# ACT's copies moved behind a period's second exp, POOL's power behind the split of x, and the scores split expert by expert, in a fused attention and expert-routing kernel

## What is computed

```
x   = _layernorm(x)                          # 16 sequences of 512 tokens, 256 wide
out = x0 + attention(x) + expert_ffn(x)      # x0 is the input
attention: q, k = rms_norm(x Wq'), rms_norm(x Wk'); v = x Wv'   # 16 heads of 16
           softmax(q k' / 4) v, then Wo'
expert_ffn: norm = layer_norm(x); scores = norm @ centroids.T    # 8192 tokens x 8 experts
           for e in 0..7: the 1024 best tokens by scores[:, e] that no expert before e has taken
           for each expert's tokens: routed + gelu(layer_norm(routed) w1 + b1) w2 + b2
           scattered back to the tokens' own rows
```

## Time and profile before

| | |
|---|---|
| median of three runs | 1113.92 us |
| the profiled execution | 1116.27 us, span 1114.5 us |
| mean granted TensorE clock | 0.979 |
| PE busy | 1052.2 us (94%) |
| DVE busy | 829.7 us (74%) |
| ACT busy | 745.0 us (67%) |
| POOL busy | 728.9 us (65%) |
| the chain that ended last | PE 69%, DVE 8%, issue 7%, POOL 5%, DMA 4%, ACT 4% |

### The profile page before, as it was taken

The page is one execution under the profiler, slowest core; times in us unless marked ns, Lnnn a source line. Parts: engine busy times, 40 slices in busy tenths (PEclk is TensorE's granted clock), DMA queues, the critical chain, the costliest instruction groups (busy, mean ns, idle before and its releaser), DMA issues.

```text
span 1114.5 us, 20949 instructions
## 1 busy us (share of the span) xinstructions
PE 1052.2 (94%) x7222; PEld 680.0 (61%) x7222; DVE 829.7 (74%) x1846; ACT 745.0 (67%) x966; POOL 728.9 (65%) x762
## 2 busy tenths in 40 slices
PE   4799999899999999999999987899999999999997
PEld 3445555444444444454454442388999889998897
DVE  8799896577777687677878787587677686776861
ACT  3488887678888878888888874675445554554550
POOL 5577877566775866777676667646676656767334
PEclk9899999999999999999999996999999999999999
DMA  4866977558577776766765966314344343444313
GB/s 142 188 143 143 219 159 154 114 132 162 125 155 148 158 138 123 179 129 139 161 136 136 166 154 129 105 57 119 81 89 122 60 119 81 85 104 77 68 20 38
DMA packets 86361, 138.16 MB, mean 124 GB/s; under 512 B 12768, under 2 KB 38624, under 8 KB 86240
## 3 DMA queue, kind: packets, MB, share of 16 engines
q1 hardware_dynamic: 57392, 103.06, 41.5%
q0 software_dynamic: 12288, 16.79, 9.0%
q10 hardware_dynamic: 16560, 16.78, 5.7%
HBM read 86.25 MB, written 50.33 MB: 123 GB/s over the span
## 4 chain that ended last, share of the span: by engine, by line
PE 69%; DVE 8%; issue 7%; POOL 5%; DMA 4%; ACT 4%; SPq 2%; ACTq 0%; POOLq 0%; another core or an unknown queue 0%; DVEq 0%
PE W L1443 16%; PE S L1429 15%; PE pv L485 13%; PE S L470 10%; PE W L431 7%; DMA stq<-parts 4%; PE W L442 3%; ACT prob L677 2%; SPq L316 2%; PE W L456 2%; DMA parts<-hi 1%; POOL hi L1186 1%; DVE raw L807 1%; PE pv L1415 1%; PE R L1415 1%
## 5 line engine op out<-in xcount | busy, mean ns | idle before, releaser
L677 ACT ACTIVATE prob<-S 128x1024 f32<-128x1024 f32 x512 | 498.1, 1022 | 132.6 <-PE S L470 131.0
L485 PE MATMUL pv<-prob,v 128*17 128x512 f32 x2048 | 252.5, 611 | 2.4 <-DVE oT L840 2.4
L470 PE MATMUL S<-stq,stk 64*128 64x512 f32 x1024 | 202.2, 460 | 24.7 <-ACT prob L677 15.4
L470 PEld LDWEIGHTS S<-stq,stk 64*128 64x128 f32 x1024 | 84.6, 186 | 150.9 <-ACT prob L677 110.5
L1705 POOL DMA_INDIRECT out<-prob,order_rows x64 | 105.8, 1653 | 48.0 <-DVE prob L1645 37.1
L485 PEld LDWEIGHTS pv<-prob,v 128*17 128x17 f32 x2048 | 48.0, 97 | 125.1 <-issue 119.2
L1156 POOL TENSOR_TENSOR sq<-raw 128x512 f32<-128x512 f32 x62 | 64.4, 1040 | 87.3 <-DVE raw L807 55.9
L1505 ACT ACTIVATE wq_act<-S,b 128x512 f32<-128x512 f32 x64 | 43.9, 687 | 94.7 <-PE S L1429 89.1
L1429 PE MATMUL S<-raw_nT,xT_w 128*128 128x512 f32 x384 | 91.1, 395 | 1.8 <-DVE raw_nT L1623 1.8
L1429 PEld LDWEIGHTS S<-raw_nT,xT_w 128*128 128x128 f32 x384 | 71.6, 188 | 19.6 <-issue 3.6
L1190 POOL TENSOR_TENSOR lo<-full,hi 128x512 fp32r<-128x512 f32 x62 | 79.9, 1289 | 5.0
(11 more groups left out here) (253 smaller groups left out, 2649.1 us busy)
## 6 DMA issues: line engine op xcount, KB each, us to landing
stk<-parts SPq DMA_DIRECT2D x192, 128.0 KB, 4.3
stq<-parts SPq DMA_DIRECT2D x192, 128.0 KB, 6.6
xT<-in_w SPq DMA_DIRECT2D x32, 512.0 KB
parts<-hi SPq DMA_DIRECT2D x63, 256.0 KB, 2.1
parts<-lo SPq DMA_DIRECT2D x63, 256.0 KB, 2.0
out<-ao ACTq DMA_DIRECT2D x32, 256.0 KB, 5.6
xb<-in_x ACTq DMA_DIRECT2D x13, 512.0 KB, 5.3
xb<-in_x SPq DMA_DIRECT2D x2, 512.0 KB, 5.7
```

The source lines that it names most:

```text
L470: ins = e.matmul(S[n % 2][:, h, :], stack["k"][u][64 * h:64 * h + 64, p, c * P:(c + 1) * P], stack["q"][u][64 * h:64 * h + 64, p, :], star ...
L485: ins = e.matmul(pv[32 * j:32 * j + VW, :], v[b % 2][:, c, 8 * u + 4 * g + j, :], prob[(2 * t + j // 2) % RING][:, j % 2, :], start=(c == ...
L677: e.activation(prob[n % RING][:, :, :], S[n % 2][:, :, :], ACT.Exp).then_inc(s_exp, 1)
```

## The change

Three things are moved, and no arithmetic is changed. On ACT, in a period, `evict_xT`, `load_x` and `evict_o` stood ahead of the period's first exp and `put_out` behind the second; now all of them stand behind the second exp, in the order second half of x, load, first half of x, output copy, output DMA. On POOL, `second_power` stood second in a period and now stands behind `split_x`. On DVE, the split of the scores' bits is made for one expert's 128x64 columns at a time: expert 0 at period 32, and the next expert's in the seventh period of each expert (`i == 6`).

```diff
@@ scalar_program @@
             for kk in range(PERIODS):
                 at = PERIODS * b + kk
-                if scored(at - 2) is not None:
-                    evict_xT(e, scored(at - 2), 0)
-                if scored(at - 3) is not None:
-                    evict_xT(e, scored(at - 3), 1)
-                    if scored(at - 3) + XB < B:
-                        load_x(e, scored(at - 3) + XB)
-                if b and kk in (5, 6):
-                    evict_o(e, b - 1, kk - 5)
                 softmax(e, 4 * at)
                 for u in range(2):
                     if nb < B and squares_at(nb, u) + 1 == at:
                         inverse_rms(e, nb, u)
                 softmax(e, 4 * at + 1)
+                if scored(at - 3) is not None:
+                    evict_xT(e, scored(at - 3), 1)
+                    if scored(at - 3) + XB < B:
+                        load_x(e, scored(at - 3) + XB)
+                if scored(at - 2) is not None:
+                    evict_xT(e, scored(at - 2), 0)
                 if b and kk in (5, 6):
+                    evict_o(e, b - 1, kk - 5)
                     put_out(e, b - 1, kk - 5)
                 softmax(e, 4 * at + 2)
                 softmax(e, 4 * at + 3)
@@ split_scores, vector_program @@
-    def split_scores(e):
+    def split_scores(e, ex):
...
-        e.tensor_scalar(word, words.bitcast(I32), 31, 1, ALU.arith_shift_right, ALU.logical_shift_right).then_inc(r_split, 1)
+        bits, words, parts = (t[:, ex, :] for t in (word, scores.bitcast(I32), part))
+        if ex == 0:
+            e.wait_ge(s_score, B)
+        e.tensor_scalar(bits, words, 31, 1, ALU.arith_shift_right, ALU.logical_shift_right).then_inc(r_split, 1)
...
                 if at == ROUTE:
-                    split_scores(e)
+                    split_scores(e, 0)
...
+                if routed(at)[1] == 6 and ex < E - 2:
+                    split_scores(e, ex + 1)
@@ gpsimd_program @@
                 if scored(at) is not None:
                     first_power(e, scored(at))
-                if scored(at - 1) is not None:
-                    second_power(e, scored(at - 1))
...
                 if b + 2 < B and kk == 5:
                     split_x(e, b + 2)
+                if scored(at - 1) is not None:
+                    second_power(e, scored(at - 1))
```

More of the change, by code:

```diff
@@ L275, in attention_and_routing @@
     hot_e = [xb[0][:, i, :].bitcast(BF16).rearrange("p (t q) -> p t q", t=COLS) for i in range(2)]
-    word = xb[0][:, 0:2, :].rearrange("p c d -> p (c d)").bitcast(I32)
-    part = xb[1][:, 0:2, :].rearrange("p c d -> p (c d)").bitcast(I32)
+    word = xb[0][:, 0:2, :].rearrange("p c d -> p (c d)").bitcast(I32).rearrange("p (e t) -> p e t", e=E)
+    part = xb[1][:, 0:2, :].rearrange("p c d -> p (c d)").bitcast(I32).rearrange("p (e t) -> p e t", e=E)
     low = xb[2][:, 0:2, :].rearrange("p c d -> p (c d)").rearrange("p (e t) -> p e t", e=E)
@@ L863, in shift_vector @@
         e.tensor_tensor(sh[1][:, :], shf[:, :], sh[0][:, :].bitcast(F32), ALU.subtract).then_inc(g_shl, 1)
-    def split_scores(e):
-        words = scores[:, :, :].rearrange("p e t -> p (e t)")
-        e.wait_ge(s_score, B)
-        e.tensor_scalar(word, words.bitcast(I32), 31, 1, ALU.arith_shift_right, ALU.logical_shift_right).then_inc(r_split, 1)
-        e.wait_ge(r_split, 1)
-        e.tensor_tensor(word, word, words.bitcast(I32), ALU.bitwise_xor).then_inc(r_split, 1)
-        e.wait_ge(r_split, 2)
-        e.tensor_scalar(part, word, LOW_BITS, None, ALU.arith_shift_right).then_inc(r_split, 1)
-        e.wait_ge(r_split, 3)
-        e.tensor_scalar(words, part, UNIT, None, ALU.mult).then_inc(r_split, 1)
-        e.tensor_scalar(word, word, 2 ** LOW_BITS - 1, None, ALU.bitwise_and).then_inc(r_split, 1)
-        e.wait_ge(r_split, 5)
-        e.tensor_copy(low[:, :, :].rearrange("p e t -> p (e t)"), word).then_inc(r_split, 1)
+    def split_scores(e, ex):
[3 more added lines that the diff above has]
+        e.tensor_scalar(bits, words, 31, 1, ALU.arith_shift_right, ALU.logical_shift_right).then_inc(r_split, 1)
+        e.wait_ge(r_split, 6 * ex + 1)
+        e.tensor_tensor(bits, bits, words, ALU.bitwise_xor).then_inc(r_split, 1)
+        e.wait_ge(r_split, 6 * ex + 2)
+        e.tensor_scalar(parts, bits, LOW_BITS, None, ALU.arith_shift_right).then_inc(r_split, 1)
+        e.wait_ge(r_split, 6 * ex + 3)
+        e.tensor_scalar(scores[:, ex, :], parts, UNIT, None, ALU.mult).then_inc(r_split, 1)
+        e.tensor_scalar(bits, bits, 2 ** LOW_BITS - 1, None, ALU.bitwise_and).then_inc(r_split, 1)
+        e.wait_ge(r_split, 6 * ex + 5)
+        e.tensor_copy(low[:, ex, :], bits).then_inc(r_split, 1)
     def ask(e, ex, i):
@@ L887, in ask @@
                 e.wait_ge(r_sel, 2 * ex)
+                e.wait_ge(r_split, 6 * ex + 6)
             e.scalar_tensor_tensor(high_key, taken[:, :], TAKEN, scores[:, ex, :], ALU.mult, ALU.add).then_inc(r_key, 1)
```

## The result

On one chip the kernel before took 1113.93 us (median of 20 runs, 1111.79 to 1117.53) and the changed one 1122.4 us (20 runs, 1117.27 to 1127.53): the medians are 8.5 us apart. The ratio measured, 1.0064 with a 95% interval of 1.0049 to 1.0079, is 7.1 us of the time before. So the change makes the kernel slower by 7 to 8.5 us. The forecast was +3.3 us, or 1117.2, within a range of 1106 to 1126, and gave "no change within 0.5%" 0.50 and "slower" 0.32: the time lies in the range, and the outcome is the second of these.

What follows compares the result with a forecast made beforehand. It took PE, busy 94% of the span, to bound the kernel. Its terms, 6.8 - 0.2 + 5.3 - 4.9 - 3.7 + 0 = +3.3 us on a median of 1113.92, gave 1117.2 us, with an 8-in-10 range of 1106 to 1126.

Steps and rivals of the forecast that it cites:

- The stall of period 30: ACT's copy of x waits for POOL's split with exps queued behind; moving it was to gain 4.9 us.
- The late copy of x: In odd scored periods PE's scores of x wait for ACT's copy: 11 x 0.62 = 6.8 us lost.
- The output pair: Output copy and its DMA together on ACT delay the next exps and PE; net 5.3 us lost.
- I take 0, with 2 to 3 us a split: DVE's six splits for later experts were to cost nothing; upper end 19 us.
- The cover: Time DVE can spend on a small split before PE waits: 4.2 us, read at the end of period 38.
- the rival of the blocked DVE: Small splits held up by POOL at six places make the kernel slower, 1125 to 1136 us; chance 0.12.
- the 3.7 us of periods 32 and 33: Splitting only an eighth of the columns at period 32 was to gain 3.7 us.
- The upper bound of 4.1: Most that the smaller split at period 32 could give: 13.69 - 9.61 = 4.1 us.
- no cost that I find: Moving POOL's power was priced at nothing, since DVE uses it two periods later.
- Either half of the change would do: In period 30, ACT's later copy or POOL's earlier split would each remove the stall.
- periods 15 and 23 at nothing: The late copy there was to be offset by a period before shortened as much: 0 us.

Runs made afterwards that it cites:

- e3_dve: The kernel before with only DVE's split of the scores made expert by expert; 1116.17 us, ratio 1.0058.
- e1_act: The kernel before with only ACT's part of the change; 1117.76 us, ratio 1.0073.
- e8_nopool: The changed kernel with POOL's power ahead of its other work again; 1116.76 us, ratio to the kernel before 1.0059.
- e7_select: The kernel before with batch 15's first copy of x behind the second exp and scores split by expert, experts 1 to 6 in kk 6; 1104.22 us, ratio 0.9933.
- e9_x15: The kernel before with only batch 15's first copy of x moved behind the second exp; 1105.84 us, ratio 0.9940.
- e11_best: The kernel before with batch 15's copy moved, small splits in kk 6, output copy behind second exp, its DMA behind the third; 1102.29 us, ratio 0.9912.
- e2_pool: The kernel before with only POOL's power moved behind the split of x; 1115.24 us, ratio 1.0050.
- e4_apart: The changed kernel with the output's DMA behind the third exp, apart from its copy; 1118.53 us, ratio to the kernel before 1.0086.
- e10_pool5: The kernel before with POOL's power behind the split of x, except in kk 5 periods, where it stayed; 1112.77 us, ratio 1.0012.
- e6_kk6: The changed kernel with the scores of experts 1 to 6 split only in kk 6 periods; 1117.37 us, ratio to the kernel before 1.0058.

## Why the prediction was off in size

The forecast had the direction, and the time within its range, and three of its terms were right in kind. It was 4 to 5 us short in the time and some 9 us short once the clock is taken out (+3.3 against +11.8 and +12.2). That the miss looks small is luck: a higher granted clock, which no term had, hid about 4 us of it.

*Right, and in its size.* The stall of period 30: 4.9 forecast, 4.9 measured. The late copy of x: 0.62 a period forecast, 0.63 to 0.66 measured; the first trace has 0.5 us more in period 7, where PE waits for the stack DMA at the end of it.

*Right in kind, too large.* The output pair: 1.10 us from copy to exp in both, and 0.5 to 0.7 a period. But it came to 3.2 us and not 5.3. Of the ten `kk` 7 that were to pay in full only eight did: period 63 kept its length, and 111 came out 0.6 shorter. Period 57 (in the first trace) and 81 came out 0.4 shorter. Period 68, 0.5 shorter, goes with DVE's part: it is so in e3_dve and not in e1_act. No run asked why these are shorter.

*Failed: "I take 0, with 2 to 3 us a split: only one of the six has two inputs, so most should be near the fast end."* This term made the largest part of the miss, +4.5 and +5.7 us in the two traces, with 1.5 more of lower clock. The cover was about right: in before, DVE is idle 1.40 us at 321.17 and has the count of period 51 ready 2.3 us early, 3.7 us for the 4.2 of period 38. The duration was not: 4.4 to 4.9 us where `kk` is 2, and 2.6 to 2.8 where it is 6. The splits stand in both kinds, and the rows that the forecast took the earlier trace rows were of the second only. It is the rival of the blocked DVE, at three of its six places. In period 51 an eighth of the columns took as long as all of them had: 4.90 us and 5.12. The one-input operations were held as long as the two-input one (1.01 us): L873 0.95 and L875 1.33 us. The sentence of the Trainium skill that the forecast leaned on (SBUF — State Buffer, section "SBUF: two separate sides") names, beside an operation with two SBUF inputs, one "in a 2-port perf mode", and the forecast left that half out. This trace agrees with the full sentence as far as it goes: one-input operations are held too, though no row shows in which mode they ran. By that sentence the pair goes to the operation that "starts first". The rows agree: each of the five POOL operations started with its DVE neighbour or up to 0.16 us ahead of it, and kept its length (1.06, 1.06, 1.29, 0.62 and 0.61 us, each the median of its line in before). So DVE lost every turn in the row.

*Failed: the 3.7 us of periods 32 and 33.* The upper bound of 4.1 was read from lengths in which 1.6 us was clock: 3.09 for 1.91 us of products and 1.17 for 0.73 us of heads in period 33. The split's share is 1.3 to 1.5 us.

*Failed: "no cost that I find" for POOL's power.* Alone it costs 5 us, within the changed kernel 0.5 (periods up to 29, without the start) to 2.6 (rest). "Either half of the change would do" for the stall fell with it. The step looked at who needs the power's result and at the time POOL spends waiting, not at what that wait kept apart. The 0.4 to 0.5 us in each of periods 5 and 6 is this, though e8_nopool paid as much in period 7 without it.

*Failed: periods 15 and 23 at nothing.* They pay 0.65 and 0.42; the period before gives back 0.2, not 0.6. The size is loose: both are 6.50 us in the changed kernel, and in the kernels with the old order there (e3_dve, e7_select, e9_x15, e11_best) they are 5.62 to 6.27 and 5.62 to 5.66.

*Not priced: the clock.* By the rest the change costs 11.7 us, and the mean time shows 7.4; the other 4.3 are the higher clock (0.9857 against 0.9817 on one chip). In the traces the difference lies in single groups of products. Periods 122 and 124, before and then after:

```profile
687.47 3.61 PE L485 MATMUL pv<-prob,v 128*17 128x512 f32 x16
...
701.67 3.50 PE L485 MATMUL pv<-prob,v 128*17 128x512 f32 x16
```

```profile
697.88 1.91 PE L485 MATMUL pv<-prob,v 128*17 128x512 f32 x16
...
708.49 1.91 PE L485 MATMUL pv<-prob,v 128*17 128x512 f32 x16
```

The Trainium skill (TensorE: Matmul & The Clock Gate, section "What's actually happening") says of the slow products at the start of a kernel that their number is "run-variable". These are in the middle, but they vary in the same way: period 122 has its 16 products at 1.91 us in one trace of the changed kernel and at 3.55, with a granted clock of 0.50, in the other. Between kernels, period 33 is slow in before and e9_x15 and fast in e2_pool. Why the share differs by up to 8 us between kernels, in both directions, stays open. e4_apart and e3_dve lost time by it, the changed kernel gained, and no experiment isolated it. The clock is what is left to say why none of the four kernels that undid a part of the change was measurably faster than the whole, although their places were 2 to 6 us shorter.

## What to carry to other kernels

A wait of one engine can be what keeps it off another's short operations: before moving it, look at what it would run, and beside what, if it did not wait. Cutting one long operation into short ones saves nothing where each short one is held until an operation of the other engine ends. A price read at one place of a pattern holds for the places that share its neighbours, so read one row of each kind. Gains at one stalled instruction are had by moving that instruction: one copy in one period gave 0.6%, while the move in every period cost 0.7% with that gain in it.

## What the runs showed of the hardware

- DVE operations of 128x4 to 128x64 take 0.16 to 0.23 us where POOL does not hold them up (e10_pool5, e6_kk6) and up to 1.36 us beside POOL, ending 0.05 to 0.08 us behind POOL's operation, also those with one input. POOL's own durations there (1.06 and 1.29 us) are the medians of the same lines in before.
- An ACT copy, a DMA that waits for it, and the next activation take 1.10 us from start to start; with the DMA behind the next exp, that exp starts after 0.48.
- After a wait of 1.98 us PE's next 16 products took 3.12 us at a granted clock of 0.59; after one of 1.78 in e9_x15, 3.09 us; after a like one (1.80 us, e10_pool5) 1.91 at a clock of 1.00. The same wait does not always lower the clock.
